# Third phase of a long two-batch MLP takes its chunks in another order; three pre-activations stay in SBUF, two pieces of VectorE's work change places

## What is computed

```python
cms_out = gelu(attn_out @ cW1 + cb1) @ cW2 + cb2
cms_out = cms_out + target_embed
concat = concatenate([attn_out, cms_out], axis=-1)
modifier = gelu(concat @ mW1 + mb1) @ mW2 + mb2
out = clip(x + cms_out + modifier, 0.0, 1.0)
```

## Time and profile before

| | us |
|---|---|
| median of 3 runs (1191.43 to 1193.93) | 1193.88 |
| the profiled execution | 1193.7 |
| its span in the profile | 1191.9 |
| TensorE busy (matmul) | 1075.9 |
| VectorE busy | 810.8 |
| ScalarE busy | 499.0 |
| mean granted TensorE clock | 0.958 |

### The profile page before, as it was taken

One profiled execution on the slowest core, in us unless ns is written; L12 is line 12 of the kernel. 1 busy time (PEld: TensorE's weight loads), 2 busy tenths in 40 slices (PEclk: granted clock), 3 DMA queues, 4 the chain that ended last, 5 costly groups with the idle time before them and its releaser, 6 DMA issues. The chain is left out here.

```text
span 1191.9 us, 13920 instructions
## 1 busy us (share of the span) xinstructions
PE 1075.9 (90%) x4985; PEld 889.5 (75%) x4985; DVE 810.8 (68%) x1413; ACT 499.0 (42%) x879; POOL 6.5 (1%) x11
## 2 busy tenths in 40 slices
PE   8996899999997799999999669999999769999955
PEld 6786688888775588887888558888877547888854
DVE  4344886767676588877335988676758548887758
ACT  4335645443352334333336445444435224443331
POOL 0000000000000000000000000000000000000000
PEclk9999899999998799999999889999999969999978
DMA  6400211211344431307304232221124443233062
GB/s 213 177 1 1 78 65 37 70 36 37 106 159 159 147 136 71 124 19 281 89 1 125 96 116 71 106 71 36 36 88 150 155 172 124 89 124 106 1 144 86
DMA packets 57246, 116.28 MB, mean 98 GB/s; under 512 B 3358, under 2 KB 32090, under 8 KB 51546
## 3 DMA queue, kind: packets, MB, share of 16 engines
q1 hardware_dynamic: 57088, 115.37, 28.8%
q10 hardware_dynamic: 90, 0.02, 0.0%
HBM read 88.12 MB, written 27.26 MB: 97 GB/s over the span
## 5 line engine op out<-in xcount | busy, mean ns | idle before, releaser
L591 ACT ACTIVATE sbc<-sbc,bias 128x512 f32<-128x512 f32 x112 | 81.1, 724 | 318.7 <-DVE sbc L889 255.6
L213 PE MATMUL bank<-ta_hi,w_lo 128*128 128x512 f32 x448 | 180.2, 402 | 37.8 <-DVE w_lo L818 20.3
L919 DVE TENSOR_TENSOR acc<-bank,acc 128x512 f32<-128x512 f32 x224 | 154.0, 687 | 87.6 <-PE bank L215 87.4
L213 PE MATMUL bank<-hid_hi,w_lo 128*128 128x512 f32 x512 | 200.3, 391 | 2.4 <-DVE acc L916 1.3
L215 PE MATMUL bank<-hid_lo,w_hi 128*128 128x512 f32 x512 | 199.3, 389 | 0.0
L214 PE MATMUL bank<-hid_hi,w_hi 128*128 128x512 f32 x512 | 199.2, 389 | 0.0
L214 PE MATMUL bank<-ta_hi,w_hi 128*128 128x512 f32 x448 | 177.5, 396 | 0.0
L215 PE MATMUL bank<-ta_lo,w_hi 128*128 128x512 f32 x448 | 177.1, 395 | 0.0
L213 PEld LDWEIGHTS bank<-ta_hi,w_lo 128*128 128x128 f32 x448 | 86.0, 192 | 64.2 <-DVE w_lo L818 21.4
L889 DVE TENSOR_TENSOR sbc<-bank,sbc 128x512 f32<-128x512 f32 x144 | 98.5, 684 | 34.7 <-PE bank L215 34.6
L213 PEld LDWEIGHTS bank<-hid_hi,w_lo 128*128 128x128 f32 x512 | 96.1, 188 | 25.7 <-issue 3.7
(11 more groups left out here) (158 smaller groups left out, 1568.0 us busy)
## 6 DMA issues: line engine op xcount, KB each, us to landing
w_raw<-in_L_cond_mW SPq DMA_DIRECT2D x48, 512.0 KB, 4.2
w_raw<-in_L_cond_cW SPq DMA_DIRECT2D x32, 512.0 KB, 4.3
pre_d<-sbc SPq DMA_DIRECT2D x16, 1024.0 KB, 4.6
sbc<-pre_d SPq DMA_DIRECT2D x16, 1024.0 KB, 7.3
x_raw<-in_x SPq DMA_DIRECT2D x4, 1024.0 KB, 6.0
e_raw<-in_L_cond_W_down SPq DMA_DIRECT2D x8, 512.0 KB, 7.9
e_raw<-in_L_cond_W_up SPq DMA_DIRECT2D x8, 512.0 KB, 3.7
proj_hi<-aw_hi SPq DMA_DIRECT2D x2, 1024.0 KB, 10.8
```

What stands on the lines that cost most here:

```text
L213: nc.tensor.matmul(dst, w_l, a_h, start=start, stop=False, **kw)
L591: nc.scalar.activation(dst, dst, ACT.Gelu, **kw).then_inc(g_done[key], 1)
L919: nc.vector.tensor_tensor(dst, bank[:, :], dst, ALU.add).then_inc(evac, 1)
```

## The change

Third phase: quad i >= 16 works on chunk (i + 5) % 8, so the order of chunks is 5, 6, 7, 0, 1, 2, 3, 4; weight columns, bias columns and DRAM slots follow that. Quads 13, 14 and 15 (chunks 5, 6, 7) are not stored any more and quads 16, 17 and 18 are not loaded: they lie in the slots 1, 2 and 0 already. Waits on the load become waits on the combinations of three quads before. In phase 1 (the weights' line has `late`) C22(it-1) stands ahead of the first low parts of the next weights. In step 15 the residual add moves behind C12(14).

```diff
+        chunk_of = lambda i: (i + NQ - 3) % NQ if i >= 2 * NQ else i % NQ
@@ dve_s_pre
-            dve.wait_ge(pre_in[i % 3], 16 * in_count(b, i))
+            if i < 2 * NQ + 3:
+                dve.wait_ge({1: c11_done, 2: c12_done, 5: c22_done}[which], g - 2)
+            else:
+                dve.wait_ge(pre_in[i % 3], 16 * in_count(b, i))
@@ dve_c21_pre
             dve.wait_ge(p4_mm, quad(b, i) + 1)
+            if i < 2 * NQ + 3:
+                dve.wait_ge(c21_done, quad(b, i) - 2)
@@ dve_mlp
-                if it + 1 < QB:
+                late = new and ph == 1
+                if it + 1 < QB and not late:
                     dve_w1_first(dve, b, it + 1)
                 down(1)
                 if old:
                     dve_c(dve, b, it - 1, "22")
-                if old and pph != 1 and it - 1 not in (-1,):
+                if it + 1 < QB and late:
+                    dve_w1_first(dve, b, it + 1)
+                if old and pph != 1:
                     dve_hid(dve, b, it - 1, "11")
...
-                elif it == 15:
-                    dve_resid(dve, b)
                 if old:
                     dve_c(dve, b, it - 1, "12")
+                if it == 15:
+                    dve_resid(dve, b)
@@ load_w1
-            c = (i % NQ) * 2 * P
+            c = chunk_of(i) * 2 * P
@@ sync_mlp
-                if 0 <= j and phase_of(j) == 1:
+                if NQ <= j < 2 * NQ - 3:
...
-                if 2 * NQ <= j < QB:
-                    if phase_of(j - 3) == 1:
-                        sp.wait_ge(pre_out[j % 3], 16 * pre_count(b, j - 3))
-                    else:
-                        for key in ("11", "12", "22", "21"):
-                            sp.wait_ge(hid_l[key], l2_of(b, j - 3) + 1)
-                    sp.wait_ge(pre_out[(j - NQ) % 3], 16 * pre_count(b, j - NQ))
-                    sp.dma_start(sbc[:, j % 3, :, :].rearrange("p c n -> p (c n)"), pre_d[j - 2 * NQ, :, :])\
+                if 2 * NQ + 3 <= j < QB:
+                    for key in ("11", "12", "22", "21"):
+                        sp.wait_ge(hid_l[key], l2_of(b, j - 3) + 1)
+                    src = NQ + chunk_of(j)
+                    sp.wait_ge(pre_out[src % 3], 16 * pre_count(b, src))
+                    sp.dma_start(sbc[:, j % 3, :, :].rearrange("p c n -> p (c n)"), pre_d[chunk_of(j), :, :])\
```

More of the change, by code:

```diff
@@ L50, in build @@
     proj_lo = nc.dram_tensor("proj_lo", (P, 2, KT * V), F32, kind="Internal").ap()
-    pre_d = nc.dram_tensor("pre_d", (NQ, P, 4 * TB), F32, kind="Internal").ap()
+    pre_d = nc.dram_tensor("pre_d", (NQ - 3, P, 4 * TB), F32, kind="Internal").ap()
     xt_d = nc.dram_tensor("xt_d", (2, P, KT * TB), F32, kind="Internal").ap()
@@ L579, in act_gelu @@
             c, t, tile = TILE[key]
-            col = (MB1 if phase_of(i) else CB1) + 2 * (i % NQ) + c
+            col = (MB1 if phase_of(i) else CB1) + 2 * chunk_of(i) + c
             kw = dict(bias=bias[:, col:col + 1])
@@ L607, in build @@
         gelu_count = lambda b, i, key: l2_of(b, i) + 1 if key != "21" else NQ * b + (i - 2 * NQ) + 1
-        pre_count = lambda b, i: sum(1 for q in range(NQ, 2 * NQ) if q % 3 == i % 3) * b + sum(
+        pre_count = lambda b, i: sum(1 for q in range(NQ, 2 * NQ - 3) if q % 3 == i % 3) * b + sum(
             1 for q in range(NQ, i + 1) if q % 3 == i % 3)
@@ L871, in dve_s_pre @@
             nc.vector.tensor_tensor(dst, ps[3 * (i % 2) + bank][:, :], dst, ALU.add).then_inc(done, 1)
-        in_count = lambda b, i: sum(1 for q in range(2 * NQ, QB) if q % 3 == i % 3) * b + sum(
-            1 for q in range(2 * NQ, i + 1) if q % 3 == i % 3)
+        in_count = lambda b, i: sum(1 for q in range(2 * NQ + 3, QB) if q % 3 == i % 3) * b + sum(
+            1 for q in range(2 * NQ + 3, i + 1) if q % 3 == i % 3)
         def dve_c21_pre(dve, b, i):
             dve.wait_ge(p4_mm, quad(b, i) + 1)
+            if i < 2 * NQ + 3:
+                dve.wait_ge(c21_done, quad(b, i) - 2)
             dst = sbc[:, i % 3, 3, :]
@@ L1257, in load_w2 @@
             src = mw2 if phase_of(i) else cw2
-            c = 2 * (i % NQ)
+            c = 2 * chunk_of(i)
             sp.dma_start(w2_raw[:, r % 2, :, :], src[:, c:c + 2, :]).then_inc(w2_in[r % 2], 16)
```

## The result

The changed kernel takes **1161.13 us** (median of 4 runs, 1160.48 to 1163.9) against 1193.68 us of the kernel before beside it (1191.43 to 1193.93): a ratio of 0.9736, with a 95% interval from 0.9716 to 0.9756. The forecast was 1164.7 with a range from 1155 to 1174. The profiled execution is the longest of the four, 1163.9 us, 0.8 under the forecast made for such an execution; the median is 3.6 under it.

What follows compares the result with a forecast made beforehand. TensorE, busy 90% of the span, was taken as the bound, with stalls behind VectorE and reloads and clock falls to win. Savings of 13.1 us (batch 0) and 15.9 (batch 1), together 29.0 off 1193.7, gave 1164.7 us; range 1155 to 1174.

Steps and rivals of the forecast that it cites:

- D1(16): Third-phase border: VectorE's addition of quad 16's first product to the pre-activation, starting at 370.84, when the residual add ends.
- p4(15): Border, TensorE's "A22 T4" product of quad 15: starts at 377.37 after a 4.4 us stall behind VectorE's row of work.
- Part 1: Second phase, C22 ahead of weight parts: turn falls from 10.26 to 8.99 us, TensorE becomes the bound; some 8.4 us.
- Rival C: Second phase: C22's move gives nothing since another link takes the loop's place; 8.4 us dearer, 1173; chance 0.07.
- Part 2: Step 15, residual add behind C12(14): delays VectorE's next addition from 368.3 to 370.84, costing 2.5 us.
- Part 3: Three pre-activations stay in SBUF: 12 of 32 transfers go, and VectorE's four reload waits, 31.3 us, vanish.
- rival D: Reload waits stay in another form, with quad 19's reload late; chance 0.01.
- The clock: Behind the border's 4.4 us stall TensorE runs at 1.2 GHz for some 10 us, from about 376.7 to 386.7.
- The place of the last stall: Before the second layer of quad 16: TensorE waits 3.0 us for hid_lo 21, until 399.2.
- Rival B: Second clock fall after the stall before quad 16's second layer: 1.7 to 4.7 us a batch, 1168 to 1174; chance 0.16.
- Rival A: Clock stays up behind the border's 4.4 us stall: 3.8 us less a batch, 1157.1; chance 0.15.
- E: Kernel gets slower: half clock holds through the dense third phase in both batches, 1212 at 100 us; chance 0.02.

Runs made afterwards that it cites:

- part 3 alone: Kernel before with only the new third-phase chunk order and three pre-activations kept in SBUF, C22 and residual add where they were: 1160.56 us, ratio 0.9716.
- parts 1 and 3: Changed kernel with the residual add put back ahead of C12(14): 1155.67 us, ratio 0.9676.
- part 2 alone: Kernel before with only the residual add moved behind C12(14), reloads still there: 1192.28 us, ratio 0.9984.

## Why the prediction came out right, step by step

The profiled execution after runs 0.3 to 0.4 us late long before the changed part, so 0.37 is taken off its times here.

| point, first batch | predicted | measured |
|---|---|---|
| p4(10) | 324.74 | 324.74 |
| p1(16) | 365.57 | 365.67 |
| residual add | 366.44 | 366.55 |
| D1(16) | 370.84 | 370.95 |
| p6(16), stall | 371.59, 0.6 | 371.69, 0.41 |
| p4(15), stall | 377.37, 4.4 | 377.47, 4.12 |
| half clock behind it | 10 us | 6.8 us |
| D1(17) | 385.5 | 384.23 |
| p4(16), stall | 392.0, nearly none | 390.76, 1.19 |
| wait before p1(18) | none | 1.90 |
| second layer of quad 16, stall | 399.2, 3.0 | 398.11, none |

- **Part 1.** The turn without the 1.27 us did come down to TensorE's own time, with no stall from p4(10) to p6(16): VectorE was its bound, C22 its gate. Rival C (nothing from part 1) is out by the kernel with it alone, at 9.0 us. What the prediction calls "of the 29.0, some 8.4 are part 1" holds only for part 1 in the kernel before; beside part 3 it is 4.9, since TensorE runs into the same VectorE chain sooner and there loses the clock.
- **Part 2.** Predicted 2.5 a batch, measured 5.5 for both together. The mechanism (add ahead of D1(16) instead of in the wait for p3(14)) is shown by the two timelines: from p7(10) to D1(16) it is 47.38 us with the add ahead and 49.90 with it behind, 2.5 as forecast. In the profiled executions p4(15) to the second layer takes 0.85 longer with the stall of 4.12 than with that of 2.31 (20.64 against 19.79), since the lower clock lasts 6.8 us instead of some 3.4.
- **Part 3.** No wait for a reload remains, the reload of quad 19 is not waited for either (rival D is out), and the part alone gives 33.6 us.
- **The clock: the term that was mis-sized.** I carried over the 10.2 us of half clock from before; it was 6.8. Matmuls are back at 0.23 us from 382.7 on, so D1(17) comes 1.3 earlier than forecast, and everything behind it too. This is most of the 1.1 us by which the second layer comes earlier in the first batch; in the second it lies 73.64 us behind p4(10), where 74.46 was forecast, so 0.8 earlier.
- **The place of the last stall.** I put 3.0 us before the second layer of quad 16, behind hid_lo. Of it 1.9 lies one product ahead, before p1(18), which needs the bank that tile 21 of quad 16 leaves (dve_c21_pre), and 1.2 before p4(16). The time of the second layer came out nearly the same, since it waits for hid_lo of the same tile: in part 3 alone it starts 2.26 us behind p1(18) (394.43 to 396.69), 0.63 of it idle behind hid_lo. It mattered for the next step: only moving dve_c21_pre took that wait away.
- **Rival B.** Its mechanism came, behind the wait for p1(18), for 3.4 us a batch instead of 4 to 10. Up to the second layer it costs 0.2 us (398.48 against 396.05 + 2.26, the distance where the clock was kept), and the three matmuls behind it at half clock 0.6: 0.8 a batch, not 1.7 to 4.7.
- **Rival A and E.** The clock did fall in the profiled execution (A is out for it), and it did not stay down (E is out). The other three runs of the changed kernel are 2.5 to 3.4 us shorter than the profiled one; a fall less in one batch would be worth 3.8 by rival A's working. Their mean granted clocks are 0.970, 0.968 and 0.967, against 0.967 for the profiled one, so for the run of 1161.41 us, with the same 0.967, the clock does not explain it. No trace shows those runs; what does stays open.
- **How much of the hit is luck.** Two sizes were off in opposite directions: the first lower stretch was too long (1.1 and 0.8 us up to the second layer), a second fall came that the forecast did not have (0.6 a batch behind that point), and this execution was 0.37 late before the border. That the sum came within 0.8 us is closer than the 3 that the prediction claimed for itself; against the median it is 3.6.

"TensorE: Matmul & The Clock Gate" of the Trainium skill, section Terms, prices the clock by half of the throttled time: an estimate of 3.4 us for the first fall and 1.7 for the second. The rows agree with it where TensorE was busy in the whole lower stretch: parts 1 and 3 lose 1.58 us from p4(15) to p4(16) (12.61 against 11.03) for its 3.2 to 3.4 us at half clock. They give the first fall here 2.3 (377.84 to 391.13 is 13.29, against 11.03), since some 2 of its 6.8 us lie in the stall, and the second 0.8, since TensorE would have waited for hid_lo anyway.

## What to carry to other kernels

Where an in-order engine waits for a transfer, long work can be put into that wait at no cost; the same place costs once the wait is gone. Moving the add behind a product's evacuation won 1.8 us while the reload was there, and cost 5.5 (10.7 without part 1) once it was gone. So whoever removes a wait has to look again at every reordering that leaned on it, and measure parts in pairs, not only alone (9.0 + 1.8 + 33.6 became 32.6; parts 1 and 2 without 3 were not run). Once the wait is gone, list the work of the waited-for engine between its input and the result that the bound engine needs, and move what nobody wants soon (here weight parts, and low parts for a later layer) behind that result, or into a wait that is there anyway (here the add). Such moves took another 18 us, more than half of the change's own gain; 5.5 of it only take back part 2, and for the split of the add by itself no gain can be told.

## What the hardware showed that was not expected

Whether the clock falls is not told by the length of the stall. Before p4(15) it stayed at 2.4 GHz behind 1.57 us (part 3 alone) and fell behind 2.31 (parts 1 and 3). Before p4(10) a wait of 1.96 us kept it in the first batch of part 3 alone and lost it in the second (PEclk 0.66 in the stretch from 880), and lost it in both batches of part 2 alone, where 1.99 had kept it in both batches of the kernel before. Before p1(18) it fell behind 1.90 in the changed kernel and was kept behind 1.91 in the first batch of parts 1 and 3, and the same wait of 2.11 us kept it in one batch and lost it in the other batch of one execution. Nor do the lower stretches have one length: before, 10.2 us in the first batch and 13.6 in the second (PEclk 0.91, 0.50, 0.50 and 0.73 from 945 to 965), each with a further stall of 2.9 inside it; 6.8 after; and several of 3.2 to 3.4. I had taken it as a fixed 10 us behind each long stall; what a stall costs in clock is better given as a range, here from 0 to some 14 us at half clock for stalls of 1.9 us and more. What decides it these runs do not show.
